# Cross attention over 1500 keys: a maximum over two key blocks from a difference product, projections two heads per product, and the maxima's row by one transpose and a DMA

## What is computed

```
for each item b and head h:                          # 32 items, 16 heads
    q  = norm(x[b]) @ Wq[:, h]                       # 56 rows
    k, v = ctx[b] @ Wk[:, h], ctx[b] @ Wv[:, h]      # 1500 keys
    p  = softmax(q @ k.T * scale)                    # over the 1500 keys
    out += (p @ v) @ Wo[h]
x = x + out + bo
```

## Time and profile before

| | |
|---|---|
| median of 3 runs | 4666.33 us (4658.75 to 4667.04) |
| the profiled execution | 4668.34 us, of which its span is 4666.5 us |
| TensorE, VectorE | busy 92% and 81% of the span |
| ScalarE, GpSimd | busy 51% and 50% |
| mean granted clock of TensorE | 0.942 of full speed |

### The profile page before, as it was taken

How to read it: one execution, slowest core, us unless ns; L and a number is a source line. 1 busy time by engine, 2 the same in 40 slices (tenths; PEclk the granted TensorE clock), 3 DMA queues, 4 the chain that set the end, 5 groups by cost and what they waited for, 6 DMA issues and landing times.

```text
span 4666.5 us, 100471 instructions
## 1 busy us (share of the span) xinstructions
PE 4313.2 (92%) x41241; PEld 2925.2 (63%) x41241; DVE 3774.7 (81%) x5349; ACT 2387.9 (51%) x4536; POOL 2319.5 (50%) x2453
## 2 busy tenths in 40 slices
PE   7999999889998999999799999996996999999968
PEld 4666666656554666666556666664664566666644
DVE  6889888757778999999789999996554899999942
ACT  3666666533344555555355656551441555555521
POOL 3888878737673545455435555553002354545520
PEclk8999999979998999999799999996997999999975
DMA  4222322013331111111001111110001011111000
GB/s 97 82 83 76 84 83 81 30 58 122 113 99 53 35 43 35 43 40 38 23 28 38 40 38 41 38 36 16 3 1 35 26 35 43 35 43 41 30 11 8
DMA packets 78147, 221.59 MB, mean 47 GB/s; under 512 B 9016, under 2 KB 14408, under 8 KB 76312
## 3 DMA queue, kind: packets, MB, share of 16 engines
q1 hardware_dynamic: 77688, 215.16, 15.4%
HBM read 158.73 MB, written 50.26 MB: 45 GB/s over the span
## 4 chain that ended last, share of the span: by engine, by line
PE 73%; DVE 14%; POOL 6%; ACT 4%; issue 2%; DMA 0%; SPq 0%; POOLq 0%; ACTq 0%; DVEq 0%
PE ps L158 70%; DVE wst L601 5%; DVE wst L621 2%; POOL wst L386 2%; POOL cx L373 2%; PE ps L498 1%; ACT wst L569 1%; ACT wst L562 1%; DVE xn L147 1%; POOL cx L380 1%; DVE st L138 1%; PE ps L197 1%; PE ps L210 1%; DVE big L978 1%; DVE x L964 1%
## 5 line engine op out<-in xcount | busy, mean ns | idle before, releaser
L569 ACT ACTIVATE wst<-ps 125x448 f32<-125x448 f32 x3072 | 1505.8, 543 | 1200.5 <-PE ps L158 1197.4
L386 POOL TENSOR_TENSOR wst<-wst 125x256 bf16<-125x256 f32 x1536 | 1137.9, 741 | 1348.6 <-ACT wst L569 1302.8
L601 DVE TENSOR_REDUCE wst<-ps 128x2 f32<-128x1000 f32 (+1 forms) x1408 | 1613.8, 1148 | 198.6 <-PE ps L158 195.1
L158 PE MATMUL ps<-big,cx 128*125 128x448 bf16 (+1 forms) x6144 | 1486.4, 360 | 0.0
L621 DVE TENSOR_TENSOR wst<-wst 125x640 bf16<-125x640 f32 x1536 | 1406.1, 916 | 59.3 <-ACT wst L569 58.1
L158 PEld LDWEIGHTS ps<-cx,wst 125*128 125x128 bf16 x23040 | 1106.9, 98 | 379.3 <-issue 51.0
L158 PE MATMUL ps<-cx,wst 125*128 125x65 bf16 (+2 forms) x23040 | 1207.8, 204 | 30.1 <-POOL wst L386 22.1
L158 PE MATMUL ps<-cx,big 128*128 128x500 bf16 (+1 forms) x3584 | 856.5, 337 | 78.0 <-DVE wst L601 61.5
L158 PEld LDWEIGHTS ps<-big,cx 128*125 128x125 bf16 (+1 forms) x6144 | 726.8, 137 | 302.5 <-issue 85.0
L158 PEld LDWEIGHTS ps<-cx,big 128*128 128x128 bf16 x3584 | 226.3, 98 | 460.8 <-DVE wst L601 351.2
L158 PE MATMUL ps<-xT,wa 128*128 128x448 f32 x640 | 299.1, 581 | 1.2 <-ACT wb L255 0.8
(11 more groups left out here) (197 smaller groups left out, 3770.7 us busy)
## 6 DMA issues: line engine op xcount, KB each, us to landing
cx<-ctxN SPq DMA_DIRECT2D x64, 377.9 KB
cTs<-in_ctxT SPq DMA_DIRECT2D x64, 375.0 KB, 5.1
cx<-in_ctxN SPq DMA_DIRECT2D x64, 375.0 KB
cx<-ctxT SPq DMA_DIRECT2D x64, 375.0 KB, 3.4
ctxN<-cx SPq DMA_DIRECT2D x32, 377.9 KB
ynN<-cx SPq DMA_DIRECT2D x32, 377.9 KB
cx<-ynN SPq DMA_DIRECT2D x32, 377.9 KB
ctxT<-cx SPq DMA_DIRECT2D x32, 375.0 KB, 6.8
```

Of the source, the lines that this page charges most:

```text
L158: return t.matmul(o, l, r, start=start, stop=stop, skip_group_check=True)
L386: g.tensor_tensor(pl[r][0:KP, at:], pf[r][0:KP, at:], pf[r][0:KP, at:].bitcast(BF16)[:, 1::2], ALU.subtract).then_inc(s["plp"], 1)
L569: e.activation(pf[T % 3][0:KP, cols], bank(2 + n2 % 3, 448)[0:KP], ACT.Exp, scale=scale).then_inc(s["ev"], 1)
L601: v.tensor_reduce(o, of, AX.X, ALU.max).then_inc(s["red"], 1)
```

## The change

Three edits, all in the cross attention.

- **Maximum over two blocks.** `diff` holds keys 0 to 499 minus keys 500 to 999. For each group of 128 query columns TensorE multiplies with `diff` and with keys 500 to 999; ScalarE writes relu of the first product to `half` (bf16), and VectorE adds the second to it and takes the maximum in one `tensor_tensor_reduce`: relu(a - b) + b is the larger of a and b. Such a unit is called "first". Keys 1000 to 1499 are reduced as before, two groups at a time ("rest"). An item keeps 21 products in 11 units: 7 first, 3 rest pairs and a rest single. VectorE makes `diff` once per item. The order within a step moves: the maximum products now stand ahead of the scores, relu ahead of the exponentials, and the reduction ahead of `pl`.
- **Projections two heads per product.** The folded weights are no longer written twice (`fold_out`), and one product gives two heads, each in 64 rows. ScalarE and VectorE still split head by head. `Qh` then misses its second copy, which `sp_double` makes by DMA, once per eight items (once for item 0 alone at the start). Projections stand at i = 0, 4 and 8, 8 per chunk in place of 16.
- **Maxima's row by one transpose.** At `due(T, -4)` one product turns `top` (128 x 7) into 7 x 128, ScalarE copies that to `topT`, and SyncE's `sp_shift` carries it to row 64 of `Ql`.

```diff
 def dve_fold / act_fold:
-                for d in range(copies):
-                    v.tensor_copy(fold_out(n)[:, per * j:per * j + per, d, :], ...)
+                v.tensor_copy(fold_out(n)[:, per * j:per * j + per, :], ...)
+        def sp_double(y, w, ci, c, first, last):
+            at = 8 * (c % 2)
+            o = slice(at + first, at + last)
+            sm = s["qd_0"] if last == 1 else s["qd_1"]
+            w.wait_ge(s["pa"], 64 * ci + 16 * (c + 1))
+            y.dma_start(Qh[64:128, o, 0:HQ // 2], Qh[0:64, o, 0:HQ // 2]).then_inc(sm, 16)
+            y.dma_start(Qh[0:64, o, HQ // 2:], Qh[64:128, o, HQ // 2:]).then_inc(sm, 16)
+        def unit(u):
+            a, i = 2 * (u // 3), u % 3
+            if u == 10:
+                return "rest", ((6, 2),)
+            return ("first", ((a, 0), (a, 1))) if i == 0 else ("first", ((a + 1, 0), (a + 1, 1))) if i == 1 else ("rest", ((a, 2), (a + 1, 2)))
+        def sp_shift(y, w, ci, k):
+            w.wait_ge(s["ev"], (2 * NT + B) * ci + 2 * max(0, KT * k - 4) + k + 1)
+            y.dma_start(Ql[64:65, k % HB, :], topT[k % 2][:, :]).then_inc(s[f"tops_{k % 2}"], 16)
 def products(k, u):
-                for n in range(2 * u, min(2 * u + 2, 21)):
-                    j, c = divmod(n, 3)
-                    r = mm(t, bank(pair_bank(k, u) + n % 2, 500), Qh[...], cs[k % 3][:, 500 * c:500 * c + 500], True, True)
+                wait_doubled(w, ci, k)
+                w.wait_ge(s["dif"], b0 + k + 1)
+                for n, (j, c) in enumerate(unit(u)[1]):
+                    r = mm(t, bank(pair_bank(k, u) + n, 500), Qh[...],
+                           diff[:, :] if c == 0 else cs[k % 3][:, 500 * c:500 * c + 500], True, True)
 def act_cross:
+                for k, u in turns(T):
+                    if unit(u)[0] == "first":
+                        q = 11 * (b0 + k) + u
+                        w.wait_ge(s["mxm"], q + 1)
+                        if q:
+                            w.wait_ge(s["red"], q - (u % 3 == 0))
+                        e.activation(half, bank(pair_bank(k, u), 500), ACT.Relu).then_inc(s["half"], 1)
 def dve_cross, reduce(k, u):
+                if kind == "first":
+                    w.wait_ge(s["half"], NJ * (b0 + k) + halves_to(u) + 1)
+                    v.tensor_tensor_reduce(out=half, in0=bank(at + 1, 500), in1=half, scale=1.0, scalar=-3.0e38,
+                                           op0=ALU.add, op1=ALU.max, accum_out=to[:, j, 0:1]).then_inc(s["red"], 1)
+                    return
 def dve_cross:
+                if (k := due(T, -17)) >= 0:
+                    v.tensor_tensor(diff[:, :], cs[k % 3][:, 0:500], cs[k % 3][:, 500:1000], ALU.subtract).then_inc(s["dif"], 1)
```

More of the change, by code:

```diff
@@ L91, in build @@
         raw = [wst[:, 4032 + 903 * i:4935 + 903 * i].rearrange("p (j c) -> p j c", j=NJ) for i in range(2)]
-        mx = [wst[:, 5838 + 21 * i:5859 + 21 * i].rearrange("p (j c) -> p j c", j=NJ) for i in range(2)]
+        mx = [wst[:, 5838 + 14 * i:5852 + 14 * i].rearrange("p (j c) -> p j c", j=NJ) for i in range(2)]
+        half = wst[:, 5872:6122].bitcast(BF16)
         top = [sb(f"top{i}", [128, NJ], BF16) for i in range(2)]
+        topT = [sb(f"topT{i}", [NJ, 128], BF16) for i in range(2)]
+        diff = sb("diff", [128, 500], BF16)
         rden = [sb(f"rden{i}", [128, NJ]) for i in range(2)]
@@ L245, in act_fold @@
                 w.wait_ge(s["f1"], jobs1[f] + j + 1)
-                for d in range(copies):
-                    e.activation(fold_out(n)[:, per * j:per * j + per, d, :],
-                                 bank(4 + j).rearrange("p (h c) -> p h c", c=n), ACT.Copy).then_inc(s["f1a"], 1)
+                e.activation(fold_out(n)[:, per * j:per * j + per, :],
+                             bank(4 + j).rearrange("p (h c) -> p h c", c=n), ACT.Copy).then_inc(s["f1a"], 1)
             for j in range(4):
@@ L279, in turns, with place, wait_doubled, halves_to @@
             return [(k, n) for n in range(11) if n * KT // 11 == r] if 0 <= k < B else []
+        def place(h):
+            return NQ * (h // 2 + H // 2 * (h % 2))
+        def sp_double(y, w, ci, c, first, last):
[5 more added lines that the diff above has]
+            y.dma_start(Qh[0:64, o, HQ // 2:], Qh[64:128, o, HQ // 2:]).then_inc(sm, 16)
+        def wait_doubled(w, ci, k):
+            if k:
+                w.wait_ge(s["qd_1"], 32 * (4 * ci + k // 8 + 1))
+            else:
+                w.wait_ge(s["qd_0"], 32 * (ci + 1))
+        def unit(u):
[3 more added lines that the diff above has]
+            return ("first", ((a, 0), (a, 1))) if i == 0 else ("first", ((a + 1, 0), (a + 1, 1))) if i == 1 else ("rest", ((a, 2), (a + 1, 2)))
+        def halves_to(u):
+            return sum(unit(i)[0] == "first" for i in range(u))
         def pair_bank(k, u):
@@ L289, in slot @@
             if i < 12:
-                return ("project", "split")[i % 2] if p < 12 and p % 4 < 3 and h < H else "", c + 1, h
+                return ("project", "split 0", "split 1", "")[i % 4] if p < 12 and p % 4 < 3 and g < H // 2 else "", c + 1, g
             if p:
@@ L331, in sp_cross @@
                     w.wait_ge(s["sc"], 2 * (t0 + KT * (k - 2)))
+                if k % 8 == 7 and k < B - 1:
+                    sp_double(y, w, ci, k // 8 + 1, 0, 8)
                 if k < B:
@@ L571, in act_cross @@
                 what, p, k = slot(T)
-                if what == "split":
-                    split(p, k)
+                if what in ("split 0", "split 1"):
+                    split(p, 2 * k + (what == "split 1"))
                 if what == "turned":
@@ L622, in dve_cross @@
                                     ALU.subtract).then_inc(s["pl"], 1)
-                for k, u in turns(T):
-                    reduce(k, u)
                 what, p, k = slot(T)
-                if what == "split":
-                    split(p, k)
+                if what in ("split 0", "split 1"):
+                    split(p, 2 * k + (what == "split 1"))
                 if what == "add":
```

130 lines of the change are left out of this document (70 added, 60 removed), and 2 rows, old and new, of the table s.

## The result

The changed kernel takes 4694.84 us (median of 4 runs, 4693.13 to 4695.82), the kernel before 4666.51 beside it: ratio 1.006, 95% interval 1.0048 to 1.0073. It is 28 us slower. I had forecast 4638, 28 us faster. The time lies in the forecast's range, next to the 4694 of the rival "dearer pair", but the pair was not dearer than I took it to be, so that rival did not come true either, and the range holds the result by luck.

What follows compares the result with a forecast made beforehand. Bare steps bound by the loop of TensorE's pair and VectorE's reduction (1.89 us), steps with more work by TensorE. Patterns -5.8, start -1, folds -0.5: -7.3 per attention, -29 in four, from 4668.3 to 4638; range 4590 to 4720.

Steps and rivals of the forecast that it cites:

- dearer pair: Rival: in first units VectorE's sum and read of the maximum take 0.82, not 0.74: +56, 4694; chance 0.27.
- Maxima's row, twice: 2.64 becomes 2.03, -1.22.: Two steps per pattern with the maxima's row shorten from 2.64 to 2.03 us each, -1.22 together.
- I cost all three at nothing: Row's DMA, SyncE's waits in `sp_shift` and the doubling of a chunk: no cost in time.
- the rival of the late transfer: Row's DMA late by 3 us for each of the first attention's 32 items: +96, 4734; chance 0.07.
- Projections, -0.75.: Projections at i = 2, 6, 10 go, 0.75 of TensorE's work each; -0.75 comes back per pattern with projections.
- About 0.5 for `diff`: VectorE's making of `diff` takes about 0.5 us per item, within an item's new total of 10.0.
- VectorE's load is no bound ... That relief is worth nothing by itself.: VectorE's reductions per item fall from 12.7 to 10.0 us, `diff` included, bringing nothing: the loop's latency was late.
- Each first unit in a bare step costs +0.14.: Loop from pair to pair through ScalarE's relu and VectorE's sum: 2.03 against 1.89, +0.14 per bare first unit.
- +0.35: Step i = 14: relu stands behind the sums' copies on ScalarE, so it lasts 3.0 instead of about 2.65.
- So -1: Start of an attention: splits -1.9, item 0's 7 first units about +1; -1 per attention.
- cheaper pair: Rival: the read costs only what VectorE hides, so the pair takes 0.69: -35, 4603; chance 0.15.
- TensorE's case (4516): Rival: TensorE binds and the loop hides, so its whole saving of 150 in four attentions comes: 4516; chance 0.04.

Runs made afterwards that it cites:

- max_row: Changed kernel with the projections of before (24 products a chunk of queries rather than 12, splits at odd steps): 4704.36 us, ratio 1.0058.
- row_first: Changed kernel with SyncE issuing the row's DMA ahead of the two stores in the first attention: 4681.98 us, ratio 1.0035.
- proj_only: Kernel before with only the projections changed (two heads a product, new splits, doubling by DMA, folds): 4661.71 us, ratio 0.9996.
- no_diff: Changed kernel with `diff` never made, first units multiplying by key block 0 instead: 4660.86 us, ratio 1.0004.
- bank_free: Changed kernel, but a unit's first product waits only for the previous relu, relu only for the first product, the sum for the second: 4589.41 us, ratio 0.9838.
- row_only: Kernel before with only the maxima's row changed (one transpose, one copy, a DMA, `top` earlier): 4636.24 us, ratio 0.9963.

## Why the prediction was wrong

The forecast's sum of -29 was made of +80 for the maximum (36 patterns of 0.84 + 0.35, 28 of 1.12 + 0.2), -72 for the row (64 patterns of 1.12), -31 for projections and turns (36 of 0.85), -4 for the starts and -2 for the folds. On the path of max_row the runs give +42, -6 and -10. The row came short by 66, projections, turns, starts and folds together by 27, and the maximum cost 38 less than forecast: 66 + 27 - 38 = 55, the whole way from -29 to +26. (The sum's last line is off by one: 4666.3 - 29.2 is 4637.) In sums over a pattern, with projections I had -0.8 and the second and fourth attention give +0.46; without them I had +0.2, and they give -0.09.

- **"Maxima's row, twice: 2.64 becomes 2.03, -1.22."** Failed, and it is the largest saving. Beside the new maximum the row's step was not 2.64 but 2.39, and became 1.99: -0.40. And the edit adds a wait: the transpose stands at the head of step 8 and `top` at the head of VectorE's step 7, so steps 7 and 19 grow from 1.84 to 2.09: +0.25. Together -0.3 a pattern instead of -1.12. The first attention adds the late DMA, so that the row's edit makes it 6.9 longer.
- **"I cost all three at nothing" (row's transfer, `sp_shift`, doubling).** Failed for the row in the first attention, 13 us (row_first). That is the rival of the late transfer at an eighth of its 96. The doubling is not free either, but small: from the last split of the start to the first maximum product it was 0.10 before in each of the three later attentions, and is 0.90, 1.27 and 0.91 in the changed kernel, some 3 in all. There the profile puts the wait down to `diff`; proj_only, which has no `diff`, shows what ends it. Most of this wait is for the splits, which the forecast had:

```profile
PE ps L162 <- DMA big<-big: 18.8, 3, 7.4
```

- **Projections, -0.75.** Failed, and in the second and fourth attention in its sign: +0.16 beside the other two edits. I counted only how much of TensorE's saving would come back, "only what does not run into the loop or into VectorE's split (0.61)", and never put the split itself on the path. It now stands ahead of a bare step. Alone the edit costs +0.4 a pattern (52.21 to 52.62 in the second and fourth attention); with the split a step later it pays. That the third attention's splits are longer is in no term of the forecast.
- **"About 0.5 for `diff`", on an engine that is no bound.** Failed, and the 0.5 had no row: between 1600 and 2100 us its median is 0.86 and its longest 1.07, and in the three later attentions some 1.0 of it is on the path in each pattern with projections: 25 us in all (no_diff).
- **"VectorE's load is no bound ... That relief is worth nothing by itself."** Failed in the kernel's favour. The earlier trace rows show it: reduction to pl 1.12, pl to reduction 0.77, in sum the 1.89 of the step, with no idle time before either. VectorE was exactly full in the very step that I read as a loop of latency. Two bounds of equal length stood there, and I saw one. So its relief may be worth something, and I take it to be the larger part of why the maximum cost 42 and not 80: a pattern grew by 0.60 with projections (52.21 to 52.81) where I had 1.19, and by 0.21 without (48.90 to 49.11) where I had 1.32. No run shows that share by itself.
- **"Each first unit in a bare step costs +0.14."** Right mechanism, size 0.10: the loop measured 1.99. Relu 0.589 for 0.58; the pair 0.68 with 0.06 to TensorE, for 0.74 with 0.05.
- **"+0.35" for relu behind the sums' copy.** Right mechanism, a larger size: steps 13 to 15, which hold pairs alone, take 6.86 for 6.34, +0.52, of which the bare step 15 has 0 and the rest is this.
- **"So -1" for the start of an attention.** Failed: from first projection to first scores 41.0, 36.0, 34.3 and 36.9 became 43.1, 39.4, 40.7 and 39.4, +14.4 in four, where some 2 us of each, one turn of the loop, are only the products of step 0, which now stand ahead of its scores. In the third some 2 more are the clock: its projections ran at a granted 1.00 before (2332 to 2346 us), where the same stretch of the changed kernel (2340 to 2354) has 0.74. In the start all of item 0's units follow each other, so the loop over ScalarE is bare there: from the first maximum product to the first scores the second attention takes 25.4 for 20.6, where I had +1; bank_free takes about 3 back in each.
- **The rival of the dearer pair** gave the right time by chance. Its test, the accumulator's read, came out on the other side: 0.68, the "cheaper pair", which would have made 4603. TensorE's case (4516) did not come, nor half speed. Of the signs that I named, relu, the read, the 2.0 from pair to pair, the 3.0 of the steps with the sums' copy (2.98) and a TensorE below 99% came. More waits for VectorE than 131 in 500 us did not: the changed kernel has 99 for the sum and 16 for its other work.
- The Trainium skill's page "VectorE: DVE Perf Modes", section "Two Vector instructions with no wait between them", says that an op which also writes its accumulator out is two instructions. The trace agrees: it shows both, and they take 0.68 together, near the 0.71 estimated from that page's section on the TRN2 errata.

## What to carry to other kernels

Before a removal is priced, list what stands on the other engines during exactly that time: the work that goes may be the cover of a split, a reduction or a DMA, and two removals may share one cover (22 us here, of the row and the projections). Check in the timeline whether the engine that ends a wait has any idle time itself; if not, it is full and not merely late. Price each instance of a repeated stage by its own rows: here the first and the third attention behaved unlike the other two. Then place what is left: one split a step later, one DMA ahead of two stores and one bank released by its own reader gave 0.9764, where the change itself gave 1.006.

## What the runs showed of the hardware

**The last 100 us have two clocks.** Behind the last attention TensorE stands idle for 23 us while VectorE works, at a granted clock of 0.50, and then runs a chain of products. Windows of that chain, in the profiled execution of the changed kernel and then of row_only (columns as in the earlier trace rows, the granted clock is the third figure from the end):

```profile
4606.00:4616.00 10.00, 9.71 (x37) 8.07 (x37) 1.46 (x4) 0.00 (x0) 0.00 (x0) 0.50 0.01 2
4616.00:4626.00 10.00, 10.00 (x16) 3.53 (x15) 1.54 (x3) 1.68 (x3) 0.00 (x0) 0.50 0.00 0
```

```profile
4593.00:4603.00 10.00, 10.00 (x39) 4.95 (x38) 2.74 (x6) 2.08 (x4) 0.00 (x0) 1.00 0.00 0
4603.00:4613.00 10.00, 9.51 (x49) 6.24 (x49) 2.40 (x6) 1.30 (x3) 0.00 (x0) 1.00 0.01 2
```

The same code ran at the level of 1.2 GHz in one and of 2.4 GHz in the other, and from the scores of the last attention's last step to the end it took 216.6 us and 176.3. Ten runs of row_only fall into two groups, six at 4632.56 to 4637.05 and four at 4671.16 to 4675.00, and its profile is one of the six. The stretches between show up elsewhere too (207.8 in proj_only and bank_free). The profile of before has 216.8, all but the same as the changed kernel's, so the comparison of those two is not touched. What decides between the two levels stays open.

**VectorE waits inside an instruction for GpSimd, by who starts first.** In the changed kernel, 1600 to 2100 us, `diff` in the view by tile (min, median, max in ns):

```profile
L665 DVE TENSOR_TENSOR diff<-cx x20: 412/863/1075, 1607.4 to 2093.3; 128x500 bf16<-128x500 bf16 x20
```

Two of the twenty on the timeline, the first behind a GpSimd instruction, the second just ahead of one:

```profile
1607.36 0.61 POOL L435 TENSOR_TENSOR wst<-wst 125x256 bf16<-125x256 f32 x1 [1.48 <-ACT wst L615]
1607.38 0.86 DVE L665 TENSOR_TENSOR diff<-cx 128x500 bf16<-128x500 bf16 x1
...
1630.56 0.41 DVE L665 TENSOR_TENSOR diff<-cx 128x500 bf16<-128x500 bf16 x1
1630.57 0.88 POOL L435 TENSOR_TENSOR wst<-wst 125x256 bf16<-125x256 f32 x1 [0.77 <-ACT wst L615]
```

Started 0.02 behind GpSimd, `diff` ends 0.27 after GpSimd's end (1607.97 to 1608.24); started 0.01 ahead of it, it takes 0.41 though GpSimd runs beside it all the while, and GpSimd's instruction takes 0.88 for the 0.61 of the first. The same holds for the 1.07 at 1735.57: GpSimd's 0.94 from 1735.44 ends at 1736.38, and `diff` 0.26 later. The Trainium skill (page "SBUF — State Buffer", section "SBUF: two separate sides") describes this, for a VectorE instruction with two inputs in SBUF beside a GpSimd instruction that reads SBUF, as an exclusive lock that the one which starts first holds for its whole instruction; these rows agree. I had priced `diff` by its elements and looked for GpSimd only as an engine that others wait for. pl is held in the same way: 0.81 on its own, 1.48 at 1608.24 beside GpSimd.
